# The waits for the last stores, issued by GpSimd instead of SyncE

## The chip, the cores and the metric

The kernel runs on one core of a Trainium2 chip. The metric is the device time of one execution in microseconds (us). The five engines of the core are TensorE (PE), VectorE (DVE), ScalarE (ACT), GpSimd (POOL) and SyncE (SP). SP computes nothing: it issues transfers and waits on semaphores.

## The reference

A batch of 128 matrices of 128 x 512 floats is multiplied, each with a 512 x 512 weight matrix chosen by its category, a bias row is added, and the input is added to the result:

```
selected_W = W[cat_ids]            # cat_ids: 128 numbers 0..30; W: 32 x 512 x 512
selected_b = b[cat_ids]            # b: 32 x 512
x = x + (einsum('bti,bio->bto', x, selected_W) + selected_b[:, None, :])   # x: 128 x 128 x 512
```

## The kernel before

Everything is in one function, `cond_resid`, as one block with a program of its own for each engine. The engines meet only through semaphores.

At the start DVE and PE sort the 128 matrices by category, so that each weight matrix is loaded once. The order is written to a table (`tbc`), from which SP reads the addresses of loads and stores.

POOL prepares the weights, one category (of 32) after the other. It loads a matrix of 128 x 2048 floats into `wr` (L213, in some turns with a piece of bias, L135), adds the identity to its diagonal (L246), which stands for the addition of x, and splits it into a high part `wh` (L254) and a low part `wl` (L258). In all it issues 29 loads of weights and 8 of bias. The last two categories load nothing more, so POOL's program ends with their L246, L254 and L258. All DMAs of POOL are software DMAs: GpSimd itself makes their descriptors.

ACT splits each matrix of x into `xh` (L284) and a copy in PSUM (L287), DVE makes the low part `xl` (L336). PE computes each of the 128 results with 12 matmuls of 128 x 128 by 512 (L411): high by high, high by low, low by high. DVE adds the bias and writes the result to one of `NO = 6` buffers `os` (L364).

SP issues the loads of x, six ahead (`AHEAD`), and the store of each result (L193), once DVE has written it. A store counts 16 on the semaphore of its buffer, `s_o[i % NO]`, when it has landed. Before a buffer is written again, DVE waits for that semaphore. The stores of the last six results have no such reader, and SP waits for them at the end of its program (L195 and L196), one wait for each of the six semaphores. Several of these waits can share one instruction: L196 has three records.

What follows the engines' programs is put there by the block itself. When the block ends, each engine executes a DRAIN, reports on a semaphore, and waits. POOL has its own DRAIN too, then waits until the other four have reported, and releases them. The records of this exit carry line L36, where the scope of the kernel opens. A similar meeting stands at the start of the program, under L438. Neither is written out in the kernel's source.

Of the kernel before, what the change touches and what calls it, by code (L numbers as in the profile page):

```python
# [5 lines left out]
def cond_resid(nc, xt, ids, W, bias, out):  # L6
# [13 lines left out]
    B, D = 128, 512  # L20
# [4 lines left out]
    NO = 6  # L25
# [10 lines left out]
    with ExitStack() as ctx:  # L36
# [3 lines left out]
        def sem(name):  # L40
            return ctx.enter_context(nc.semaphore(name))
# [48 lines left out]
        s_o = [sem(f"s_o{i}") for i in range(NO)]  # L90
# [26 lines left out]
        def chunk(c, k0, k1):  # L117
            return slice(slot(c) + k0 * D, slot(c) + k1 * D)

        def raw(c, k0, k1):  # L120
            return wr[:, c % NR, k0 * D:k1 * D]

        def diagonal(c, k0, k1):

            t = wr[:, c % NR, k0 * D + k0 * 128:]
            return bass.AP(t.tensor, t.offset, [list(t.ap[0]), [D + 128, k1 - k0], [1, 128]])

        def ones_on(n):

            t = ident[:, :]  # L130
            return bass.AP(t.tensor, t.offset, [list(t.ap[0]), [0, n], [1, 128]])

        def bias_load(eng, j0, j1, done):
            at = slice(j0 * D, j1 * D)
            eng.dma_start(bb[:, at].rearrange("p (c d) -> p c d", c=j1 - j0),  # L135
                          bias[j0:j1, :].rearrange("(a c) d -> a c d", a=1).to_broadcast([128, j1 - j0, D]))\
               .then_inc(done, 16)

        def table(eng, name, src, n, lo, hi, ahead=8):

            regs = [eng.alloc_register(f"{name}{i}") for i in range(ahead)]

            def get(i):
                if i % ahead == 0:
                    m = min(ahead, n - i)
                    eng.load(regs[:m], src[0:1, i:i + m])
                return eng.snap(regs[i % ahead], min_val=lo, max_val=hi)
            return get

        def x_load(eng, i, b):  # L150
            eng.dma_start(xs[:, i % NX, :, :], xt[b, :, :].rearrange("a p (k t) -> (a p) k t", k=KT))\
               .then_inc(s_x[i % NX], 16)

        @block.sync
        def _(eng):
            eng.dma_start(idr[:, :], ids.rearrange("(a n) -> a n", a=1)).then_inc(s_id, 16)
            def w1_load(h):
                k0, k1 = W1[h]
                eng.dma_start(raw(1, k0, k1), W[1, :, k0 * D:k1 * D]).then_inc(s_w1[h], 16)

            first = eng.alloc_register("first")
            eng.wait_ge(s_t0, 1)
            eng.load(first, low1[0:1, 0:1])
            x_load(eng, 0, bass.ds(eng.snap(first, min_val=0, max_val=C * B - 1) % B, 1))
            w1_load(0)
            eng.wait_ge(s_tab, 1)
            ahead = table(eng, "la", tbc, B, 0, B - 1)
            behind = table(eng, "st", tbc, B, 0, B - 1)
            ahead(0)

            def load(i):
                b = ahead(i)
                if i == NX:
                    eng.wait_ge(s_xl, 2)
                elif i > NX:
                    eng.wait_ge(s_pt, i - NX)
                x_load(eng, i, bass.ds(b, 1))

            for i in range(1, AHEAD):
                load(i)  # L180
                if i == 3:
                    bias_load(eng, 0, 1, s_b0[0])
                    w1_load(1)
                if i == 4:
                    for k0, k1 in ((k, k + 1) for k in range(KT)):
                        eng.wait_ge(s_wd, k1)
                        eng.dma_start(raw(2, k0, k1), W[2, :, k0 * D:k1 * D]).then_inc(s_w2, 16)
            bias_load(eng, 1, 2, s_b0[1])
            for i in range(B):
                if i + AHEAD < B:  # L190
                    load(i + AHEAD)
                b = behind(i)
                eng.dma_start(out[bass.ds(b, 1), :, :].rearrange("a t d -> (a t) d"), os[:, i % NO, :])\  # L193
                   ._wait_ge(s_fin, i + 1).then_inc(s_o[i % NO], 16)
            for i in range(B - NO, B):  # L195
                eng.wait_ge(s_o[i % NO], 16 * (i // NO + 1))  # L196

        @block.gpsimd
        def _(eng):
            eng.iota(iot[:, :], [[1, 128]], base=0, channel_multiplier=0,  # L200
                     allow_small_or_imprecise_dtypes=True).then_inc(s_io, 1)
            eng.memset(ident[:, :], 0.0).then_inc(s_cst, 1)
            eng.wait_ge(s_cst, 1)
            eng.affine_select(out=ident[:, :], in_=ident[:, :], compare_op=ALU.not_equal, fill=1.0,
                              base=0, pattern=[[-1, 128]], channel_multiplier=1).then_inc(s_cst, 1)
            eng.iota(dif[:, :], [[-1, 128]], base=0, channel_multiplier=1,
                     allow_small_or_imprecise_dtypes=True).then_inc(s_io, 1)
            eng.iota(num[:, 0:1], [[1, 1]], base=0, channel_multiplier=1,
                     allow_small_or_imprecise_dtypes=True).then_inc(s_io, 1)
            eng.iota(thr[:, :], [[B, C]], base=B, channel_multiplier=0,  # L210
                     allow_small_or_imprecise_dtypes=True).then_inc(s_io, 1)
            def load(c):
                eng.dma_start(wr[:, c % NR, :], W[c, :, :]).then_inc(s_wr[c % NR], 16)  # L213
                if c % NB == 0:
                    bias_load(eng, c, c + NB, s_bb[c // NB])

            eng.sem_inc(s_w, 1)
            eng.wait_ge(s_cst, 2)
            for k in range(KT):
                eye = diagonal(0, k, k + 1)  # L220
                eng.wait_ge(s_w0[k // 2], 16)
                eng.tensor_tensor(eye, eye, ones_on(1), ALU.add).then_inc(s_ri, 1)  # L222
            done = table(eng, "dn", tn, C, 1, B + 1)
            eng.wait_ge(s_wd, KT)
            for h, (k0, k1) in enumerate(W1):
                half = raw(1, k0, k1)
                at = chunk(1, k0, k1)
                eye = diagonal(1, k0, k1)
                eng.wait_ge(s_w1[h], 16)
                eng.tensor_tensor(eye, eye, ones_on(k1 - k0), ALU.add).then_inc(s_ri, 1)  # L230
                eng.wait_ge(s_ri, KT + 1 + h)
                eng.tensor_scalar(wh[:, at], half, 1.0, 1.0, ALU.mult, ALU.mult).then_inc(s_wh, 1)
                eng.wait_ge(s_wh, 1 + h)
                eng.tensor_tensor(wl[:, at], half, wh[:, at].bitcast(f32), ALU.subtract).then_inc(s_wp, 1)  # L234
            eng.wait_ge(s_wp, 2)
            eng.wait_ge(s_b0[1], 16)
            eng.sem_inc(s_w, 1)
            load(3)
            bias_load(eng, 2, NB, s_bb[0])
            for c in range(2, C):  # L240
                if c == 2:
                    eng.wait_ge(s_w2, 32)
                else:
                    eng.wait_ge(s_wr[c % NR], 16 * ((c - 1) // NR))
                eye = diagonal(c, 0, KT)
                eng.tensor_tensor(eye, eye, ones_on(KT), ALU.add).then_inc(s_ri, 1)  # L246
                at = chunk(c, 0, KT)
                if c == NW:
                    eng.wait_ge(s_tab, 3)
                if c >= NW:  # L250
                    n = done(c - NW)
                    eng.wait_ge(s_mm, n).then_inc(s_free, 1)
                eng.wait_ge(s_ri, KT + 1 + c)
                eng.tensor_scalar(wh[:, at], wr[:, c % NR, :], 1.0, 1.0, ALU.mult, ALU.mult).then_inc(s_wh, 1)  # L254
                eng.wait_ge(s_wh, c + 1)
                if c % NB == 0:
                    eng.wait_ge(s_bb[c // NB], 16)
                eng.tensor_tensor(wl[:, at], wr[:, c % NR, :], wh[:, at].bitcast(f32),  # L258
                                  ALU.subtract).then_inc(s_wp if c == 2 else s_w, 1)
                if c == 2:  # L260
                    eng.wait_ge(s_wp, 3)
                    eng.wait_ge(s_bb[0], 16)
                    eng.sem_inc(s_w, 1)
                if c + NR < C:
                    eng.wait_ge(s_w, c + 1)
                    load(c + NR)

        @block.scalar
        def _(eng):
# [175 lines left out]
```

## Time and profile before

| | us |
|---|---|
| median of 3 executions | 360.77 |
| range | 360.77 to 362.27 |
| profiled execution, device time | 360.85 |
| its span, first to last instruction | 359.1 |
| TensorE's granted clock, mean | 1.00 of full speed |

The profile is of one execution. Its span runs from the first to the last instruction of the program; the device time is that of the whole execution and is 1.75 us longer. Busy times count work on the engine's datapath. Semaphore, branch, drain and DMA-issuing instructions are records of the engine's sequencer (marked with a q: POOLq, SPq) and are not counted as busy; they can be looked up by their line. A record of a sequencer instruction gives its start and its length.

### The profile page before, as it was taken

To read this page: it belongs to the slowest core of one execution; us is meant where nothing else is said; L and a number is where in the kernel's file an instruction comes from. 1 tells how busy PE (TensorE), PEld (TensorE's weight loads), DVE (VectorE), ACT (ScalarE), POOL (GpSimd) and SP (SyncE) were. 2 spreads that over 40 slices of the span, in tenths; PEclk is the share of its full clock that TensorE was granted. 3 is DMA by queue.
4 is the path that set the end of the run, shared out by engine and by line. 5 is a ranking of instruction groups with operands and counts; after the bars stand their busy time and mean duration, and the time that the engine had idled before them with its cause. 6 is when DMAs were issued, how large, how long until landed. Compare 5 with 4: busy or idle time off the path is not lost.

```text
span 359.1 us, 6771 instructions
## 1 busy us (share of the span) xinstructions
PE 353.7 (99%) x1553; PEld 289.5 (81%) x1553; DVE 172.9 (48%) x277; ACT 146.8 (41%) x263; POOL 269.2 (75%) x147
## 2 busy tenths in 40 slices
PE   7999999999999999999999999999999999999996
PEld 3888888888888888888888888888888888888884
DVE  7565455444544544544454454454445445445442
ACT  5464344434433343443443343344344243434420
POOL 4688999997747698799965999799979799934000
PEclk9999999999999999999999999999999999999999
DMA  7999998999886989899997899989998999966532
GB/s 258 296 382 375 401 380 296 304 379 348 306 314 226 356 308 327 283 326 378 321 316 267 300 379 310 333 283 379 329 328 269 352 376 305 326 204 192 182 116 88
DMA packets 43668, 109.49 MB, mean 305 GB/s; under 512 B 4849, under 2 KB 4850, under 8 KB 39026
## 3 DMA queue, kind: packets, MB, share of 16 engines
q1 hardware_dynamic: 38018, 69.75, 54.4%
q0 software_dynamic: 5328, 38.28, 30.7%
q10 hardware_dynamic: 288, 1.05, 0.9%
q8 instruction: 17, 0.28, 0.3%
q14 instruction: 17, 0.14, 0.1%
HBM read 75.50 MB, written 33.55 MB: 304 GB/s over the span
## 4 chain that ended last, share of the span: by engine, by line
PE 98%; DVE 1%; issue 0%
PE pA L411 97%; PE pA L371 1%; DVE os L364 0%; DVE below L323 0%; DVE cmp L318 0%; DVE rank L320 0%; DVE hot L321 0%; PE pS L384 0%; DVE fill L305 0%; DVE colf L316 0%; PE pS L379 0%; DVE unit L307 0%; PE pS L378 0%; DVE num L322 0%; DVE ones L306 0%
## 5 line engine op out<-in xcount | busy, mean ns | idle before, releaser
L364 DVE TENSOR_TENSOR os<-pA,bb 128x512 f32<-128x512 f32 x128 | 88.5, 691 | 171.8 <-PE pA L411 170.4
L284 ACT ACTIVATE xh<-xs 128x512 fp32r<-128x512 f32 x127 | 80.3, 632 | 195.3 <-PE pA L411 129.4
L258 POOL TENSOR_TENSOR wl<-wr,wh 128x2048 fp32r<-128x2048 f32 x30 | 138.7, 4623 | 2.5
L411 PE MATMUL pA<-wh,xh 128*128 x512 | 137.2, 389 | 0.0
L411 PE MATMUL pA<-wl,xh 128*128 x512 | 137.0, 389 | 0.0
L411 PE MATMUL pA<-wh,xl 128*128 x512 | 137.0, 389 | 0.0
L411 PEld LDWEIGHTS pA<-wh,xh 128*128 128x128 f32 x512 | 96.0, 188 | 20.1
L411 PEld LDWEIGHTS pA<-wh,xl 128*128 128x128 f32 x512 | 96.0, 188 | 20.2 <-DVE xl L331 0.3
L411 PEld LDWEIGHTS pA<-wl,xh 128*128 128x128 f32 x512 | 96.1, 188 | 20.0
L336 DVE TENSOR_TENSOR xl<-pT,xh 128x512 fp32r<-128x512 f32 x127 | 86.6, 682 | 9.2 <-ACT pT L287 9.2
L254 POOL TENSOR_SCALAR wh<-wr 128x2048 fp32r<-128x2048 f32 x30 | 57.6, 1920 | 36.9 <-PE pA L411 35.1
L287 ACT ACTIVATE pT<-xs 128x512 f32<-128x512 f32 x127 | 74.0, 583 | 0.0
L246 POOL TENSOR_TENSOR wr<-wr,ident 128x512 f32<-128x512 f32 x30 | 39.2, 1305 | 0.7
L213 POOL DMA_DIRECT2D wr<-w x29 | 17.2, 593 | 10.1 <-POOL wl L258 8.0
L371 PE MATMUL pA<-fill 128*128 128x512 bf16 x12 | 4.7, 522 | 2.0 <-DVE unit L307 1.6
L222 POOL TENSOR_TENSOR wr<-wr,ident 128x128 f32<-128x128 f32 x4 | 2.7, 694 | 3.1 <-DMA wr<-w 3.1
L234 POOL TENSOR_TENSOR wl<-wr,wh 128x1024 fp32r<-128x1024 f32 x2 | 4.8, 2404 | 0.2
L135 POOL DMA_DIRECT2D bb<-bias x8 | 4.3, 533 | 0.0
L230 POOL TENSOR_TENSOR wr<-wr,ident 128x256 f32<-128x256 f32 x2 | 1.5, 740 | 3.5 <-DVE wl L341 1.9
L371 PEld LDWEIGHTS pA<-fill 128*128 128x128 bf16 x12 | 1.1, 113 | 3.6 <-issue 3.2
L291 ACT ACTIVATE wh<-wr 128x512 fp32r<-128x512 f32 x4 | 2.3, 618 | 2.2 <-POOL wr L222 2.2
L341 DVE TENSOR_TENSOR wl<-wr,wh 128x512 fp32r<-128x512 f32 x4 | 2.8, 750 | 0.3 <-ACT wh L291 0.3
(40 smaller groups left out, 13.2 us busy)
## 6 DMA issues: line engine op xcount, KB each, us to landing
xs<-xt SPq DMA_DIRECT2D x128, 256.0 KB, 5.2
out<-os SPq DMA_DIRECT2D x128, 256.0 KB, 4.9
wr<-w POOLq DMA_DIRECT2D x29, 1024.0 KB, 7.2
bb<-bias POOLq DMA_DIRECT2D x7, 1024.0 KB, 9.7
wr<-w ACTq DMA_DIRECT2D x2, 512.0 KB, 4.4
wr<-w SPq DMA_DIRECT2D x2, 512.0 KB, 5.7
wr<-w SPq DMA_DIRECT2D x4, 256.0 KB, 6.7
bb<-bias SPq DMA_DIRECT2D x2, 256.0 KB, 6.2
```

The source lines that it names most:

```text
L135: eng.dma_start(bb[:, at].rearrange("p (c d) -> p c d", c=j1 - j0), bias[j0:j1, :].rearrange("(a c) d -> a c d", a=1).to_broadcast([128, j ...
L213: eng.dma_start(wr[:, c % NR, :], W[c, :, :]).then_inc(s_wr[c % NR], 16)
L234: eng.tensor_tensor(wl[:, at], half, wh[:, at].bitcast(f32), ALU.subtract).then_inc(s_wp, 1)
L246: eng.tensor_tensor(eye, eye, ones_on(KT), ALU.add).then_inc(s_ri, 1)
L254: eng.tensor_scalar(wh[:, at], wr[:, c % NR, :], 1.0, 1.0, ALU.mult, ALU.mult).then_inc(s_wh, 1)
L258: eng.tensor_tensor(wl[:, at], wr[:, c % NR, :], wh[:, at].bitcast(f32), ALU.subtract).then_inc(s_wp if c == 2 else s_w, 1)
L284: eng.activation(xh[:, i % NH, :, :], xs[:, i % NX, :, :], ACT.Copy).then_inc(s_xh, 1)
L287: eng.activation(pT[i % NT][:, :, :], xs[:, i % NX, :, :], ACT.Copy).then_inc(s_pt, 1)
L336: eng.tensor_tensor(xl[:, i % NH, :, :], pT[i % NT][:, :, :], xh[:, i % NH, :, :].bitcast(f32), ALU.subtract).then_inc(s_xl, 1)
L364: eng.tensor_tensor(os[:, i % NO, :], pA[i % NA][:, :], bb[:, bass.ds(at, D)], ALU.add)._wait_ge(s_mm, i + 2).then_inc(s_fin, 1)
L371: eng.matmul(pA[0][:, :], fill[:, 0:128], fill[:, :], start=True, stop=True)
L411: mm = eng.matmul(pA[i % NA][:, :], xp[:, i % NH, k, :], wp[:, bass.ds(at + k * D, D)], start=(n == 0), stop=(n == 3 * KT - 1))
```

## The change

The loop of six waits is taken out of SP's program, and the same loop is put at the end of POOL's, behind the last turn over the categories. The waits, their semaphores and their values are the same. SP's program now ends with its last store.

```diff
--- before.py
+++ after.py
@@ -192,8 +192,6 @@
                 b = behind(i)
                 eng.dma_start(out[bass.ds(b, 1), :, :].rearrange("a t d -> (a t) d"), os[:, i % NO, :])\
                    ._wait_ge(s_fin, i + 1).then_inc(s_o[i % NO], 16)
-            for i in range(B - NO, B):
-                eng.wait_ge(s_o[i % NO], 16 * (i // NO + 1))
 
         @block.gpsimd
         def _(eng):
@@ -264,6 +262,8 @@
                 if c + NR < C:
                     eng.wait_ge(s_w, c + 1)
                     load(c + NR)
+            for i in range(B - NO, B):
+                eng.wait_ge(s_o[i % NO], 16 * (i // NO + 1))
 
         @block.scalar
         def _(eng):
```

## Rows read from the trace of the kernel before

**Rows 1.** The page: busy time by engine, and the chain that ended last.
```profile
span 359.1 us, 6771 instructions
...
PE 353.7 (99%) x1553; PEld 289.5 (81%) x1553; DVE 172.9 (48%) x277; ACT 146.8 (41%) x263; POOL 269.2 (75%) x147
...
PE 98%; DVE 1%; issue 0%
```

**Rows 2.** Timeline, DVE, 355 to 360 us: start us, length us, engine, line, operation.
```profile
355.85 0.69 DVE L364 TENSOR_TENSOR os<-pA,bb 128x512 f32<-128x512 f32 x1 [2.03 <-PE pA L411]
```

**Rows 3.** The stores' line L193, 354 to 360 us: durations ns, starts us; then landing.
```profile
L193 SPq DMA_DIRECT2D out<-os x2: 332/332/333, 353.8 to 356.6; - x2
...
DMA to landing us min/median/max: 2.0/2.0/2.0
```

**Rows 4.** Waits of SP's queue, whole span: us in total, times, longest.
```profile
SPq L196 <- DMA out<-os: 1.5, 1, 1.5
```

**Rows 5.** The line of the moved waits, L196: durations ns, first and last start us.
```profile
L196 SPq EVENT_SEMAPHORE  x3: 17/28/28, 356.9 to 358.6; - x3
```

**Rows 6.** The line of the block's end, L36: the same columns.
```profile
L36 POOLq EVENT_SEMAPHORE  x2: 17/17/17, 358.9 to 358.9; - x2
L36 POOLq DRAIN  x1: 7777/7777/7777, 322.6 to 322.6; - x1
L36 ACTq DRAIN  x1: 1102/1102/1102, 345.1 to 345.1; - x1
...
L36 DVEq DRAIN  x1: 730/730/730, 355.9 to 355.9; - x1
L36 SPq COMPARE_BRANCH  x1: 38/38/38, 358.7 to 358.7; - x1
L36 SPq DRAIN  x1: 7/7/7, 358.8 to 358.8; - x1
L36 SPq EVENT_SEMAPHORE  x1: 17/17/17, 359.0 to 359.0; - x1
...
L36 PEldq EVENT_SEMAPHORE  x1: 51/51/51, 359.0 to 359.0; - x1
```

**Rows 7.** Timeline, POOL, 299 to 360 us.
```profile
299.75 4.62 POOL L258 TENSOR_TENSOR wl<-wr,wh 128x2048 fp32r<-128x2048 f32 x1
304.67 0.58 POOL L213 DMA_DIRECT2D wr<-w  x1 [0.30 <-POOL wl L258]
...
308.68 4.62 POOL L258 TENSOR_TENSOR wl<-wr,wh 128x2048 fp32r<-128x2048 f32 x1
313.25 1.30 POOL L246 TENSOR_TENSOR wr<-wr,ident 128x512 f32<-128x512 f32 x1
...
322.65 4.62 POOL L258 TENSOR_TENSOR wl<-wr,wh 128x2048 fp32r<-128x2048 f32 x1
```

**Rows 8.** POOL's load issues, line L213, 290 to 360 us; then landing.
```profile
L213 POOL DMA_DIRECT2D wr<-w x2: 583/590/596, 295.7 to 304.7; - x2
...
DMA to landing us min/median/max: 7.1/7.7/8.3
```

**Rows 9.** Timeline, ACT, 345.5 to 360 us.
```profile
345.56 0.58 ACT L287 ACTIVATE pT<-xs 128x512 f32<-128x512 f32 x1
```

**Rows 10.** DMA view, 320 to 335 us: every queue with traffic, packets, MB, share.
```profile
q1 hardware_dynamic: 1605, 2.90, 62.4%
```

**Rows 11.** The program's start, line L438 on POOL: durations ns, starts us.
```profile
L438 POOLq DRAIN  x1: 186/186/186, 0.3 to 0.3; - x1
...
L438 POOL MEMSET const-uint8-127<- x1: 101/101/101, 0.4 to 0.4; 128x1 uint8 x1
```

**Rows 12.** The page: DMA issues of POOL by line, with their count.
```profile
L213 POOL DMA_DIRECT2D wr<-w x29 | 17.2, 593 | 10.1 <-POOL wl L258 8.0
...
L135 POOL DMA_DIRECT2D bb<-bias x8 | 4.3, 533 | 0.0
```

## The prediction

> **What bounds the kernel now.** I read the page's chain of waits first: PE's matmuls of L411 are 98% of the span, DVE 1% [rows 1]. So for 350 us nothing on SP or POOL sets the pace, and a change of who waits at the end can only count behind the last matmul. The next view is therefore the timeline of the end [rows 2]: the last evacuation runs on DVE from 355.85 for 0.69, to 356.54. SP issues the last store at 356.6, and it lands 2.0 us later [rows 3], at 358.6. SP's own waits [rows 4] show 1.5 us in which L196, the loop that the change moves, waits for that landing; the last record of L196 stands at 358.6 [rows 5]. The span ends at 359.1. Between lie 0.5 us, which the records of L36, the end of the block, fill [rows 6]: SP's branch at 358.7, SP's DRAIN at 358.8 (7 ns), two 17 ns semaphore records on POOL at 358.9, and one record on each of the other four at 359.0. In this exit every engine has one DRAIN (those of POOL, ACT, DVE and SP are shown); POOL's two records come once the other four have reported, and release them. POOL's own DRAIN is long past: it starts at 322.6 and takes 7777 ns, to 330.4 [rows 6].
>
> That DRAIN is what matters here. It is 28.5 us ahead of 358.9, so in the kernel before its length is worth nothing. In the changed kernel it stands behind the waits.
>
> **The change, part by part.**
>
> Removed from SP: six waits. SP then leaves right after its last issue (356.6, 0.4 us at most), takes its branch and its 7 ns DRAIN, and reports near 357.2 instead of 358.8. Nobody but the exit waits for SP. Worth nothing by itself, since the exit now waits for POOL.
>
> Added to POOL: the same six waits, behind L258, its last operation (start 322.65, 4.62 us, to 327.27) [rows 7]. Nothing stands behind them on POOL but the block's end: its last DMA issue is at 304.7 [rows 8], no store or load of another queue is passed, and what PE needs of POOL is signalled by L258's own completion. From 322.65 to 358.6 POOL's sequencer is parked, which costs no one. The wait itself is no dearer there than on SP: POOL's semaphore records are 17 ns, SP's 17 to 28 ns [rows 5, 6].
>
> Moved by consequence: POOL's DRAIN. It can't begin at 322.6 now, only once the last landing has released the waits at 358.6. What of its 7.78 us comes back there? Up to 327.27 the engine was still in L258, so 327.27 - 322.6 = 4.7 us of the record only covers that operation. The remainder, 330.4 - 327.27 = 3.1 us, ran with POOL idle. For comparison ACT's DRAIN ends at 345.1 + 1.102 = 346.2, its last operation at 345.56 + 0.58 = 346.14; DVE's ends at 355.9 + 0.73 = 356.6, its last operation at 356.54 [rows 2, 6, 9]. These are tails of 0.1 us or less; POOL's is 3.1.
>
> Is the tail a property of the drain, or a leftover of something in flight? In the stretch 320 to 335 the DMA view has one queue with traffic, SP's q1: no software queue, no instruction loads [rows 10]. POOL's last transfer was issued at 304.7 and takes 8.3 us at most, so it had landed by 313.0 [rows 8]. No other engine sends POOL anything. So the drain waits for no transfer and no code. At the start of the program POOL has another DRAIN, 186 ns from 0.3, which ends at 0.5 with the last memset (0.4 + 0.1) [rows 11]: a tail of under 0.1 us. What differs between the two is that POOL has issued 29 + 8 = 37 DMAs in between [rows 12]. My reading is that POOL's drain goes over its issued software DMAs one after the other, whether or not they have landed: 3.1 / 37 is 84 ns for each, an estimate from these rows that no row shows alone. Then the tail is paid whenever the drain comes, with idle engine too.
>
> The cost on the path: 3.1 us, as the value of the nearest row. Its bounds: below, the first drain's tail, under 0.1 us, against which the skipped hop from SP to POOL and SP's branch (0.2 us from 358.7 to 358.9) can stand as a gain, so -0.2. Above, the whole record, 7.8 us. I take 3.1 because the part under L258 is explained by L258.
>
> A rule of the Trainium skill speaks against this. The trace shows a DRAIN that goes on 3.1 us after its engine's last operation [rows 6, 7]; the page PSUM — Partial Sum Buffer, section Engine vs sequencer instructions, says that "drain waits for the engine to go fully idle", and nothing of a cost beyond. By that rule a drain on an engine idle for 31 us is free and the kernel stays at 360.8; by the row it costs 3.1. The row is of this kernel, so I go by it, and keep the rule's outcome as the second rival.
>
> The other parts of the exit stay: from the landing, 358.6, two to three small sequencer steps to the DRAIN (SP takes 0.2 for them), then POOL's two records and the releases (0.2). SP's 7 ns DRAIN and its report are replaced by POOL's own. I put the difference at 0, give or take 0.1.
>
> **The sum**, against the profiled execution: span 359.1 + 3.1 = 362.2. Around the span lay 360.85 - 359.1 = 1.75 us, which nothing here touches: 362.2 + 1.75 = 363.95. The profiled execution is 0.08 above the median of 360.77, so the forecast for the median is 363.9, 0.9% slower. A difference under 0.5% (1.8 us) can't be told from none here.
>
> **The rivals.**
>
> 1. The whole 7.78 us belong to the drain: it goes over the 37 entries from its start on (210 ns each), beside L258 and not after it. The record can't tell this from the forecast, since it only shows start and end. For it: the two are alike if one loop does all. Against it: ACT's and DVE's drains begin under a running operation as well and end with it, so idling is the first thing they wait for. 359.1 + 7.8 = 366.9, with the 1.75 around and less 0.08: 368.6.
>
> 2. No change: the 3.1 us were POOL's settling after its last operations (retiring buffers, writes of the 128x2048 tile), which goes on without a drain as well and is over long before 358.6. Then the drain at 358.8 has a tail like the first one, under 0.1. Place: POOL's DRAIN between 358.8 and POOL's release; price 3.1 us back against the forecast; it decides as soon as POOL has been idle for more than 3.1 us ahead of the drain, and here it is 31. For it: the drain at the start and those of ACT and DVE. Against it: each of the other L258s is followed by a next operation within 0.1 to 0.3 us (299.75 + 4.62 = 304.37, next issue 304.67; 308.68 + 4.62 = 313.30, next at 313.25) [rows 7], so no unfinished write of the tile holds the engine for 3 us. Time: 360.8, and 360.6 if SP's hop (0.2) is gained. It is also where the skill's rule leads.
>
> 3. The exit gets a gain that can be measured, over 1.8 us. The whole stretch from landing to end is 0.5 us, so it isn't there; only chance could show one.
>
> That the change doesn't do what it says is hardly open: the last store's landing at 358.6 still has to be waited for by someone, and the exit joins all engines.
>
> **How the numbers follow.** Forecast 0.66. Rival 1: 0.07. Rival 2: 0.24. The remaining 0.03 are for what no row suggests: 0.01 faster, 0.01 each for a tail of some other length on either side of 0.5%. Slower: 0.66 + 0.07 + 0.01 = 0.74; same: 0.24 + 0.01 = 0.25; faster: 0.01. The forecast alone would range from 363.3 to 364.5: 0.1 us of rounding in the rows, the 0.1 of the exit's steps, and some 0.4 in which the median of a few runs may sit off. It holds only 0.66, so the range goes down to rival 2: 360.6 to 364.5 leaves out rival 1 and little else.
>
> **What would show it.** In the changed kernel's records of the block's end POOL's DRAIN starts at 358.7 to 358.9 and takes 3.1 us (3.0 to 3.2); POOL's two semaphore records stand at 361.9 to 362.1; SP's DRAIN stands near 357.1; the span is 362.2, and everything up to 356.5 (PE's 353.7 busy, the last evacuation at 355.8) is as before. A DRAIN under 0.2 us and a span of 359.0 would make rival 2 right, one of 7.7 rival 1. The prediction is also wrong if the last evacuation moves by more than 0.3 us, since then something in the loop changed that I hold untouched.

## The result, and the profile after

| | before | after |
|---|---|---|
| median of the runs, us | 360.95 (6 runs) | 364.18 (6 runs) |
| lowest, us | 360.77 | 363.87 |
| profiled execution, device time, us | 360.85 | 364.25 |
| its span, us | 359.1 | 362.5 |

The ratio is 1.0083, with a 95% interval from 1.006 to 1.0107: the changed kernel is 0.8% slower. Here and below, ratio and interval come from the single runs of both kernels and need not be the quotient of the two medians.

The page of the changed kernel, its head, its busy times and the row of the granted clock in 40 slices:

```profile
span 362.5 us, 6771 instructions
...
PE 353.9 (98%) x1553; PEld 289.4 (80%) x1553; DVE 172.6 (48%) x277; ACT 146.8 (41%) x263; POOL 269.2 (74%) x147
...
PEclk9999999999999999999999999999999999999998
```

PE's 353.9 us of work are those of before (353.7) [rows 1]. The page's chain of waits ends, in both kernels, with the last evacuation on DVE, so neither the last landing nor a DRAIN shows in it; that stretch has to be read from the records. The span is 3.4 us longer, so the difference lies where PE has nothing to do. The records of the block's end (engine, operation, count: duration in ns min/median/max, first and last start in us):

```profile
L36 POOLq EVENT_SEMAPHORE  x2: 17/17/17, 362.3 to 362.4; - x2
L36 ACTq DRAIN  x1: 1102/1102/1102, 345.4 to 345.4; - x1
...
L36 DVEq DRAIN  x1: 730/730/730, 356.2 to 356.2; - x1
L36 SPq DRAIN  x1: 129/129/129, 357.3 to 357.3; - x1
L36 POOLq COMPARE_BRANCH  x1: 33/33/33, 359.0 to 359.0; - x1
L36 POOLq DRAIN  x1: 3092/3092/3092, 359.1 to 359.1; - x1
L36 SPq EVENT_SEMAPHORE  x1: 17/17/17, 362.4 to 362.4; - x1
...
L36 PEldq EVENT_SEMAPHORE  x1: 51/51/51, 362.4 to 362.4; - x1
```

Against [rows 6], POOL's DRAIN has moved from 322.6 to 359.1, and its record has shrunk from 7777 to 3092 ns, because no operation runs under it any more: 7777 - 3092 = 4685 ns, and from 322.6 that leads to 327.3, where the last operation ended (327.27) [rows 7]. The branch with the last wait on it is now POOL's. SP's DRAIN is at 357.3, 1.5 us earlier than before, and has no effect: POOL's two records stand at 362.3 and 362.4, right behind its own DRAIN (359.1 + 3.1 = 362.2).

The moved waits, now at L266 on POOL, and the last store:

```profile
L266 POOLq EVENT_SEMAPHORE  x3: 17/43/43, 353.5 to 358.9; - x3
```

```profile
L193 SPq DMA_DIRECT2D out<-os x2: 332/332/332, 354.2 to 356.9; - x2
...
DMA to landing us min/median/max: 2.0/2.0/2.0
```

The store is issued at 356.9 and lands 2.0 us later, at 358.9, where the last record of L266 starts. On POOL the records of the waits are 17 to 43 ns long, on SP 17 to 28 [rows 5]: no difference that counts.

POOL's last operation and DVE's last evacuation, from the timeline:

```profile
322.97 4.63 POOL L256 TENSOR_TENSOR wl<-wr,wh 128x2048 fp32r<-128x2048 f32 x1
```

```profile
356.16 0.69 DVE L364 TENSOR_TENSOR os<-pA,bb 128x512 f32<-128x512 f32 x1 [2.03 <-PE pA L411]
```

POOL's last operation ends at 322.97 + 4.63 = 327.6, so POOL was idle for 31 us when the DRAIN began, and still took 3.09 us over it. The last evacuation is at 356.16, 0.31 later than in [rows 2]. So the 3.4 us of the two spans are 3.1 us of drain and 0.3 us from earlier in the program.

Those 0.3 us are there in the first 30 us, while the first loads come in (the evacuation near 29 us starts at 29.45 before and 29.76 after). The evacuation near 57 us, of before and then of after:

```profile
56.65 0.69 DVE L364 TENSOR_TENSOR os<-pA,bb 128x512 f32<-128x512 f32 x1 [1.43 <-PE pA L411]
```

```profile
56.96 0.69 DVE L364 TENSOR_TENSOR os<-pA,bb 128x512 f32<-128x512 f32 x1 [1.43 <-PE pA L411]
```

From there on the two run in step: 0.31 at 57 us and 0.31 at 356 us.

### The profile page after: what moved, and what is told of

Same layout as the page of the kernel before. It is cut to its first block, busy times and chain, and to the rows that moved or that the text cites. A ratio compares the mean times of both kernels' runs of the same rounds, so it can differ in the third digit from the quotient of the medians.

```text
span 362.5 us, 6771 instructions
## 1 busy us (share of the span) xinstructions
PE 353.9 (98%) x1553; PEld 289.4 (80%) x1553; DVE 172.6 (48%) x277; ACT 146.8 (41%) x263; POOL 269.2 (74%) x147
## 3 DMA queue, kind: packets, MB, share of 16 engines
q0 software_dynamic: 5328, 38.28, 30.4%
## 4 chain that ended last, share of the span: by engine, by line
PE 97%; DVE 1%; issue 0%
PE pA L411 96%; PE pA L371 1%; DVE os L364 0%; DVE below L323 0%; DVE cmp L318 0%; DVE rank L320 0%; DVE hot L321 0%; PE pS L384 0%; DVE fill L305 0%; DVE colf L316 0%; PE pS L379 0%; DVE unit L307 0%; PE pS L378 0%; DVE num L322 0%; DVE ones L306 0%
```

## The experiments

Three theories were on the table for the 3.1 us: (A) the drain goes over the software DMAs issued since the last drain, (B) it goes over all of the program's, (C) it costs a fixed time once software DMAs have been used. All seven experiments were timed beside runs of the kernel before on the same chip.

### A drain ahead of the waits

```diff
+            eng.drain()
             for i in range(B - NO, B):
                 eng.wait_ge(s_o[i % NO], 16 * (i // NO + 1))
```

> The changed kernel with one more line: POOL executes a DRAIN of its own ahead of the six waits, so that one DRAIN falls at about 323 us, where POOL has nothing else to do, and the block's own follows behind the last landing. Theory A (the drain goes over the software DMAs issued since the last drain, 84 ns each): the first takes 7.8 us of record (4.7 under the last operation and 3.1 behind it), the block's own under 0.1 us; span 359.1 to 359.4, time 360.9, as before the change. Theory B (it goes over all 37 DMAs of the program each time): both have a tail of 3.1 us, time 364.2. Theory C (a fixed 3.1 us once software DMAs have been used, whatever came since): as B, 364.2.

Measured: 361.14 us (before 360.92), ratio 0.9999 (0.9981 to 1.0017). The block's end on POOL, and then the DRAIN that was added (L265):

```profile
L36 POOLq EVENT_SEMAPHORE  x2: 17/17/17, 359.5 to 359.6; - x2
...
L36 POOLq COMPARE_BRANCH  x1: 33/33/33, 359.3 to 359.3; - x1
L36 POOLq DRAIN  x1: 41/41/41, 359.4 to 359.4; - x1
```

```profile
L265 POOLq DRAIN  x1: 7788/7788/7788, 323.2 to 323.2; - x1
```

The added DRAIN takes 7788 ns from 323.2, as the block's own did before the change, and the block's own, at 359.4, takes 41 ns. With the same 37 DMAs in the program, a drain with none issued since the last one is nearly free, as A has it. B and C, by which both drains have a tail of 3.1 us, fall. This run doesn't exclude that a drain is cheap merely because one came before it; the last experiment tests that. The change keeps its six waits on POOL here, and no cost shows within the interval, which is about 0.2% (0.6 us) either way.

### The waits on ACT

```diff
-        (end of POOL's program)
+        (end of ACT's program, behind its last high(i))
             for i in range(B - NO, B):
                 eng.wait_ge(s_o[i % NO], 16 * (i // NO + 1))
```

> The six waits stand at the end of ACT's program instead of POOL's. ACT issues hardware DMAs alone (two) and its DRAIN had a tail under 0.1 us in the kernel before. Theory A, B and C alike (the cost is POOL's drain, not the move off SP): ACT's DRAIN near 359.0 takes under 0.1 us, POOL's starts near 322.6 with 7.8 us of record and is hidden, time 360.9. Rival (any engine but SP pays when it waits for landings last, through a slower wake-up or hop): 362 or more.

Measured: 361.04 us, ratio 1.0002 (0.9984 to 1.0019).

```profile
L36 POOLq EVENT_SEMAPHORE  x2: 17/17/17, 359.0 to 359.1; - x2
L36 POOLq DRAIN  x1: 7797/7797/7797, 322.8 to 322.8; - x1
...
L36 ACTq DRAIN  x1: 8/8/8, 359.0 to 359.0; - x1
```

ACT's DRAIN behind the landing takes 8 ns. POOL's is back at 322.8, under its last operation and PE's work. So taking the waits off SP costs nothing as such: of SP, ACT and POOL only POOL pays. DVE and PE were not tried.

### Twice the weight DMAs

```diff
-                eng.dma_start(wr[:, c % NR, :], W[c, :, :]).then_inc(s_wr[c % NR], 16)
+                for p in (0, 64):
+                    eng.dma_start(wr[p:p + 64, c % NR, :], W[c, p:p + 64, :]).then_inc(s_wr[c % NR], 16)
...
-                    eng.wait_ge(s_wr[c % NR], 16 * ((c - 1) // NR))
+                    eng.wait_ge(s_wr[c % NR], 32 * ((c - 1) // NR))
```

> The changed kernel with each weight load of POOL split into two DMAs of 64 partitions: 58 + 8 = 66 software DMAs instead of 37, with the same bytes and about the same number of descriptors that carry data. Theory A or B by count: the block's DRAIN takes 66 x 84 ns = 5.5 us, time 364.2 + 2.4 = 366.6. By bytes or data descriptors: 3.1 us, 364.2. A fixed cost: 3.1 us, 364.2. POOL's extra issues (29 x 0.6 us = 17 us spread over the run, against 36.9 us of idle time in front of L254) should not reach PE; if they do, the last evacuation moves and only the DRAIN's record counts.

Measured: 382.0 us (380.06 to 384.5), ratio 1.0573 (1.0527 to 1.0619).

```profile
L36 POOLq DRAIN  x1: 5460/5460/5460, 374.5 to 374.5; - x1
```

5460 ns where 5.5 us were expected by count. The time was not as expected (366.6). The DMA view (queue: packets, MB, share of the 16 engines; then the issues, KB each, median us to landing):

```profile
q0 software_dynamic: 5792, 38.28, 38.5%
...
xs<-xt SPq DMA_DIRECT2D x128, 256.0 KB, 8.5
...
wr<-w POOLq DMA_DIRECT2D x58, 512.0 KB, 8.3
```

The same 38.28 MB take 38.5% of the DMA engines' time over a span of 380.2 us, in the changed kernel 30.4% of 362.5 us: 146 us instead of 110. A load of x lands in 8.5 us where it took 4.9 in the changed kernel (5.2 in the kernel before). PE's waits (us in total, times, longest) have a row that both of those lack, for the low part of x:

```profile
PE pA L412 <- DVE xl L337: 8.7, 7, 3.9
```

Against the changed kernel the span is 17.7 us longer, and the rows account for it: the last evacuation starts 15.4 us later (371.53 instead of 356.16), and the DRAIN is 2.4 us longer. The 15.4 us are PE's, which waits 12.1 us in all instead of 2.1 and is busy for 359.3 us instead of 353.9. Why halves of 64 partitions take the DMA engines more time no run shows. The time of this kernel tells nothing of the drain; its record does. Packets rose by 9% (5792 against 5328) and bytes not at all, while the DMAs rose by 78% and the DRAIN by 77%: it goes by DMAs, not by bytes or by all packets. The 464 packets more are 16 for each of the 29 DMAs more, so a cost for each DMA can't be told from a cost for 16 packets that every DMA has beside its data.

### Seven DMAs fewer on POOL

```diff
 (POOL's load(c))
-                if c % NB == 0:
-                    bias_load(eng, c, c + NB, s_bb[c // NB])
 (SP's loop over i)
                 if i + AHEAD < B:
                     load(i + AHEAD)
+                for c in range(NB, C, NB):
+                    if i == max(4, 4 * c - 24):
+                        bias_load(eng, c, c + NB, s_bb[c // NB])
```

> The changed kernel with seven of POOL's eight bias loads issued by SP: 30 software DMAs instead of 37. Theory A or B by count: the block's DRAIN takes 30 x 84 ns = 2.5 us, time 363.6. By a fixed cost: 3.1 us, 364.2. If the bias loads in SP's queue hold up a load of x, the last evacuation moves, and only the DRAIN's record counts.

Measured: 364.32 us (363.34 to 365.02), ratio 1.0078 (1.0053 to 1.0103).

```profile
L36 POOLq DRAIN  x1: 2520/2520/2520, 359.8 to 359.8; - x1
```

2520 ns, as expected by count (2.5), not by a fixed cost (3.1). The three kernels lie on one line: (3092 - 2520) / 7 = 82 ns for each DMA, and (5460 - 3092) / 29 = 82 ns, with 3092 - 37 x 81.7 = 69 ns left over. This line is of the weight and bias loads of these kernels, 0.5 or 1 MB each. The whole time does not show the 0.6 us saved: in the profiled execution the last evacuation starts at 356.78, 0.6 us later than in the changed kernel. Whether the bias loads in SP's queue did that or chance is open.

### POOL waits for the last result, SP for the landing

```diff
 (end of POOL's program in the kernel before; SP keeps the six waits)
+            eng.wait_ge(s_fin, B)
```

> The kernel before (SP waits for the landings) with one wait more at the end of POOL's program, for the last result of DVE instead of for its landing. POOL's DRAIN then starts near 356.7, ahead of the landing at 358.6. If the tail is 3.1 us from the moment that POOL comes to its DRAIN, it ends near 359.8 and SP's report (358.8) is no longer the last: the exit ends near 360.0, span +0.9 us, time 361.7. If what costs is that a landing releases POOL (rival), nothing changes: 360.9.

Measured: 362.14 us (before 360.86), ratio 1.0033 (1.0021 to 1.0046).

```profile
L36 POOLq EVENT_SEMAPHORE  x2: 17/17/17, 359.9 to 360.0; - x2
...
L36 POOLq COMPARE_BRANCH  x1: 33/33/33, 356.6 to 356.6; - x1
L36 POOLq DRAIN  x1: 3092/3092/3092, 356.8 to 356.8; - x1
...
L36 SPq DRAIN  x1: 7/7/7, 358.9 to 358.9; - x1
```

POOL comes to its DRAIN at 356.8, behind the last evacuation and ahead of the landing, and takes the same 3092 ns; SP's report at 358.9 is no longer the last. No landing releases POOL here, so the wait for a landing is not what costs. The span is 360.1, 1.0 us longer than before, where 0.9 was expected (the exit ended at 360.1, not 360.0). The median of 362.14 is 0.4 above the 361.7 expected, the profiled execution (361.86) 0.2.

### No drain on POOL

```diff
-        block = ctx.enter_context(nc.Block())
+        block = ctx.enter_context(nc.Block(no_gpsimd_drain=True))
```

> The changed kernel with the block opened so that POOL has no DRAIN in its exit; the six waits stay on POOL. If the DRAIN is the whole of the 3.1 us, they go: span 359.1, time 360.9. If something else on POOL goes over the DMAs between the waits and its two semaphore records, 364.2 stays.

Measured: 360.84 us, ratio 1.0006 (0.9989 to 1.0022).

```profile
L36 POOLq EVENT_SEMAPHORE  x2: 17/17/17, 358.9 to 358.9; - x2
...
L36 SPq DRAIN  x1: 130/130/130, 357.0 to 357.0; - x1
L36 POOLq COMPARE_BRANCH  x1: 33/33/33, 358.7 to 358.7; - x1
```

With the six waits on POOL and its DRAIN gone, POOL's branch at 358.7 is followed by its two records at 358.9, as in the kernel before. The DRAIN is the whole of the 3.1 us. The exit differs in one more way: each of the other four engines has two semaphore records on L36 instead of one, the first at its own exit and so off the path. Here all of POOL's DMAs had long landed; what it risks to leave the drain out where they have not, no run shows.

### A drain midway

```diff
                 if c + NR < C:
                     eng.wait_ge(s_w, c + 1)
                     load(c + NR)
+                if c == 16:
+                    eng.drain()
```

> The changed kernel with a DRAIN of POOL behind the load issued in turn c = 16, when 16 weight and 5 bias DMAs have been issued; 13 weight and 3 bias DMAs follow it, 16 in all. The runs so far give a block's DRAIN of 69 ns + 81.7 ns for each DMA (30: 2520, 37: 3092, 66: 5460). If only the DMAs since the last drain count, the last takes 0.07 + 16 x 0.0817 = 1.4 us: time 360.9 + 1.3 = 362.4. If a drain late in the program is simply cheap once one has been done, 0.04 us and 360.9. If all count, 3.1 and 364.2. The midway one should last until the load just issued has landed, some 7 us, if a drain also waits for transfers in flight; POOL's idle time in front of L252 should hold that.

Measured: 362.21 us, ratio 1.0033 (1.0019 to 1.0047). The block's end on POOL; the added DRAIN (L266); the load issued just before it, with its time to landing:

```profile
L36 POOLq EVENT_SEMAPHORE  x2: 17/17/17, 360.2 to 360.3; - x2
...
L36 POOLq DRAIN  x1: 1375/1375/1375, 358.8 to 358.8; - x1
```

```profile
L266 POOLq DRAIN  x1: 10107/10107/10107, 174.5 to 174.5; - x1
```

```profile
L211 POOL DMA_DIRECT2D wr<-w x1: 593/593/593, 174.6 to 174.6; - x1
...
DMA to landing us min/median/max: 9.2/9.2/9.2
```

The block's DRAIN takes 1375 ns; the line gives 69 + 16 x 81.7 = 1376. It counts the DMAs since the last drain, those alone. With none since the last drain it took 41 ns (the first experiment), a little less than the line's 69. The added one lasts from 174.5 to 184.6, and the load issued at 174.6 lands at 183.8: in this one record the drain of POOL also waits for the software transfer in flight, since by count alone it would have lasted 1.8 us. It ends 0.8 us behind that landing, less than those 1.8 us for its 21 DMAs, so a part of the walk probably lay under the transfer; that part is argued, not shown.

## Why the prediction was right

- **Nothing changes ahead of the exit, and SP's early leave is worth nothing.** Right: SP's DRAIN moved to 357.3 and nobody gained by it. The text took that DRAIN to stay at 7 ns; it took 129, which had no effect either. What PE does was as before but for 0.3 us, taken up below.
- **POOL's tail of 3.1 us is the drain's own and comes back whole behind the landing.** Right: 3.1 us by the rows of before, 3.09 us measured. The step that carried this was to count only the part of the 7777 ns that lay behind the end of the last operation. Rival 1, the walk beside the operation, would have made it 7.7 us; the DRAIN with nothing under it takes 3.09.
- **84 ns for each of 37 DMAs.** It was an estimate from one record, with no fixed part; four counts on one line (16, 30, 37, 66) make it 82 ns with 0.07 us fixed. That the length goes by the count is shown. That the drain goes over the DMAs one after the other is the picture that fits it; no record shows what it does for each. The recorded text did not say that only the DMAs since the last drain count; that came from the experiments.
- **Rival 2, leftover work that POOL would have finished by itself.** It had 0.24. POOL was idle for 31 us and the tail was there in full, so it falls. The rule of the Trainium skill that led there (PSUM — Partial Sum Buffer, section Engine vs sequencer instructions: a drain waits until the engine is idle) agrees with the trace as far as it goes: the tail of 3092 ns begins where the last operation ends. On POOL it is not the whole, since a drain that began on an engine idle for 31 us still took those 3092 ns.
- **The sum.** Forecast 363.9, measured 364.18; lowest to lowest it is 363.87 - 360.77 = 3.1 us, the term of the sum. The profiled spans differ by 3.4 instead of 3.1, and POOL's DRAIN (359.1) and its two records (362.3 and 362.4) stand 0.2 to 0.3 us behind the windows that the text gave them, as the last evacuation does.
- **What the text named as a sign against itself.** It said the prediction would be wrong if the last evacuation moved by more than 0.3 us, and it moved by 0.31. By its own words this sign speaks against the prediction, by 0.01 us. The bound was set too tight: the three executions of before already lay 1.5 us apart. The kernel with the drain midway has the same program as the changed one up to 174 us and on the other engines throughout, and its last evacuation, and that of the kernel with the drain ahead, stand here:

```profile
355.82 0.69 DVE L366 TENSOR_TENSOR os<-pA,bb 128x512 f32<-128x512 f32 x1 [2.03 <-PE pA L413]
```

```profile
356.45 0.69 DVE L365 TENSOR_TENSOR os<-pA,bb 128x512 f32<-128x512 f32 x1 [2.03 <-PE pA L412]
```

These are 355.82 and 356.45, either side of 356.16 and of the 355.85 of before, and the kernel without POOL's drain, which has the changed program up to the exit, has 355.85. Of the kernel before, 24 executions on one chip have spans from 359.0 to 361.1 us, and the shortest span of the changed kernel (362.1) is 3.1 us above the shortest of before (359.0). So the start differs by some tenths from one execution to the next, and what the change costs is the drain. What makes the start differ was not traced.

## What to carry to other kernels

On the engine that issues software DMAs, a drain cost 82 ns for each one issued since the last drain (16 to 66 of them here), even when all had long landed. Leave that engine's exit where other work covers it, and let an engine without software DMAs wait for the last landing (SP and ACT did so here at no cost). If POOL has to be the last, give it a drain of its own ahead of the final wait: here that took the whole 3.1 us off the path, and brought the kernel level with the one before, not ahead of it.

## What else the runs showed

- The mean granted clock of the changed kernel (0.997 against 1.00) is no slowdown of its matmuls. By stretch of the changed kernel (us, then busy time of PE, PEld, DVE, ACT and POOL, then the granted clock, DMA share and GB/s):

```profile
300.00:355.00 55.00, 55.00 (x244) 45.57 (x243) 24.91 (x39) 19.27 (x35) 20.84 (x8) 1.00 0.59 205
355.00:359.10 4.10, 1.12 (x5) 0.58 (x4) 0.69 (x1) 0.00 (x0) 0.00 (x0) 1.00 0.34 126
359.10:362.50 3.40, 0.00 (x0) 0.00 (x0) 0.00 (x0) 0.00 (x0) 0.00 (x0) 0.67 0.00 0
```

The clock is 1.00 as long as PE works and falls behind it, in the idle stretch that the longer exit adds to the mean. The 0.67 there is a mean between the two levels, 1.00 (2.4 GHz) and 0.50 (1.2 GHz).

- SP's DRAIN takes 129 ns right behind its last DMA issue (357.3), and 7 ns where waits for the landing lie between (358.8) [rows 6]. With 256 stores and loads behind it, its hardware queue costs it no more than that. Nor does it wait for them: in the changed kernel the last store lands at 358.9, 1.5 us after this DRAIN has ended. On SP a drain does not stand in for the waits that the change moved.
- Splitting POOL's 1 MB loads into halves of 64 partitions each cost 4.9% against the changed kernel (382.0 against 364.18), of which the longer DRAIN is 2.4 us; the 5.7% above are against the kernel before. The same bytes took 146 us of the DMA engines' time instead of 110.
